# Moving two dense products, two splits and one group of transposes in a one-core recommendation kernel

## The reference, cut to what matters

```python
fm = emb_table[arange(26), cat_idx]                  # 26 looked-up rows of 128
dense = relu(relu(relu(x @ Wd1) @ Wd2) @ Wdf)        # biases left out here
Z = concat([fm, dense])                              # 27 x 128 per batch row
S = einsum("bie,bje->bij", Z, Z)                     # all products of pairs
x = concat([S[upper triangle], dense])               # 351 + 128
x = relu(x @ Wt1 + bt1)                              # 1024 wide
x = relu(x @ Wt2 + bt2)                              # 1024
x = relu(x @ Wt3 + bt3)                              # 512
x = relu(x @ Wt4 + bt4)                              # 256
out = sigmoid(x @ Wo + bo)
```

## Time and profile before

| quantity | value |
|---|---|
| median of three runs | 179.01 us (178.82 to 179.12) |
| span of the profiled execution, first to last instruction | 176.7 us |
| TensorE busy (matmul) | 160.0 us, 91% of the span |
| GpSimd busy | 102.6 us, 58% |
| VectorE busy | 71.1 us, 40% |
| ScalarE busy | 55.1 us, 31% |
| granted TensorE clock, mean | 0.981 |

### The profile page before, as it was taken

How to read it: one execution, slowest core, us unless ns; L and a number is a source line. 1 busy time by engine, 2 the same in 40 slices (tenths; PEclk the granted TensorE clock), 3 DMA queues, 4 the chain that set the end, 5 groups by cost and what they waited for, 6 DMA issues and landing times.

```text
span 176.7 us, 3837 instructions
## 1 busy us (share of the span) xinstructions
PE 160.0 (91%) x1681; PEld 115.5 (65%) x1681; DVE 71.1 (40%) x131; ACT 55.1 (31%) x93; POOL 102.6 (58%) x111
## 2 busy tenths in 40 slices
PE   1999997449889999999999999899999998999983
PEld 1334454225657878767787877677878776788971
DVE  5005358806869624162504122734121264321311
ACT  3378588431737403032211113231113041201110
POOL 3777777777778877777777777777777000000000
PEclk9999999975999999999999999999999999999999
DMA  2999556767987522222121212222221000000000
GB/s 52 318 389 270 163 157 178 207 194 242 342 235 261 165 51 57 54 58 55 49 59 48 58 50 59 48 59 52 56 56 52 15 4 0 0 0 4 0 0 0
DMA packets 6674, 18.18 MB, mean 103 GB/s; under 512 B 2309, under 2 KB 2441, under 8 KB 6530
## 3 DMA queue, kind: packets, MB, share of 16 engines
q1 hardware_dynamic: 3330, 11.12, 19.1%
q0 software_dynamic: 3328, 6.82, 15.3%
HBM read 17.93 MB, written 0.00 MB: 101 GB/s over the span
## 4 chain that ended last, share of the span: by engine, by line
PE 68%; POOL 13%; DVE 7%; issue 5%; DMA 3%; ACT 2%; DVEq 0%
PE mp L444 26%; POOL rows L312 13%; PE mp L465 10%; PE mp L413 9%; PE gp L377 6%; PE tp L421 5%; PE gp L367 4%; PE gp L483 3%; DVE xb L717 3%; PE mp L348 2%; DMA rows<-in_emb,row_of 2%; PE mp L506 1%; DVE raw L750 1%; PE gp L389 1%; ACT xth L581 1%
## 5 line engine op out<-in xcount | busy, mean ns | idle before, releaser
L312 POOL DMA_INDIRECT rows<-in_emb,row_of x104 | 101.7, 978 | 33.2 <-issue 29.6
L444 PE MATMUL mp<-w2l,a1h 128*128 128x512 f32 x64 | 26.7, 418 | 0.0
L444 PE MATMUL mp<-w2h,a1h 128*128 128x512 f32 x64 | 26.2, 410 | 0.0
L444 PE MATMUL mp<-w2h,a1l 128*128 128x512 f32 x64 | 25.5, 398 | 0.0
L570 ACT COPY zt<-gp 128x512 f32<-128x512 f32 x16 | 9.4, 586 | 46.6 <-PE gp L367 46.5
L367 PE MATMUL gp<-ident,rows 128*128 128x128 f32 x104 | 16.4, 278 | 5.4 <-DMA rows<-in_emb,row_of 5.4
L367 PEld LDWEIGHTS gp<-ident,rows 128*128 128x128 f32 x104 | 12.8, 142 | 10.4 <-DMA rows<-in_emb,row_of 6.5
L739 DVE TENSOR_TENSOR raw<-mp,bc 128x512 f32<-128x512 f32 x8 | 5.5, 690 | 29.4 <-PE mp L444 29.4
L377 PEld LDWEIGHTS gp<-zt 128*32 128x32 f32 x1024 | 11.4, 112 | 6.9 <-issue 6.0
L377 PE MATMUL gp<-zt 128*32 128x27 f32 x1024 | 13.5, 198 | 0.6 <-DVE zt L711 0.6
L444 PEld LDWEIGHTS mp<-w2h,a1l 128*128 128x128 f32 x64 | 12.1, 189 | 2.9 <-DVE a1l L733 0.9
(11 more groups left out here) (78 smaller groups left out, 231.2 us busy)
## 6 DMA issues: line engine op xcount, KB each, us to landing
w<-in_wt SPq DMA_DIRECT2D x13, 512.0 KB, 4.5
rows<-in_emb,row_of POOLq DMA_INDIRECT x104, 2.8
w<-in_wt SPq DMA_DIRECT2D x3, 468.0 KB
bc<-in_rows SPq DMA_DIRECT2D x1, 1024.0 KB, 7.0
wd_sb<-in_wd SPq DMA_DIRECT2D x1, 512.0 KB, 3.6
w1d<-in_wt SPq DMA_DIRECT2D x1, 512.0 KB, 6.7
bt<-in_rows SPq DMA_DIRECT2D x1, 512.0 KB, 9.2
wdf_sb<-in_wdf SPq DMA_DIRECT2D x1, 128.0 KB, 3.1
```

The lines of the kernel that those rows point to most:

```text
L312: pool.indirect_dma_start(out=rows[:, n % RING, :], out_offset=None, in_=emb.rearrange("c v e -> (c v) e"), in_offset=bass.IndirectOffsetO ...
L444: last = pe.matmul(mp[:, h, :], a[:, k, :], w[:, k, cols], start=(k == 0 and part == 0), stop=(k == M1 - 1 and part == 2))
```

## The change

The change has four parts.

1. **Dense products 6 and 7** go ahead of the transposes of tile 0's groups 6 and 7 on TensorE. On VectorE their bias additions go ahead of `features(0, 7)` and `turn_sums(0)`.
2. **Group 6** of each next tile goes from behind layer 3 into it, ahead of product 14. Group 7 stays behind layer 3.
3. **Group 5 and grams 2** go to earlier places in layer 3: ahead of products 4 and 10 in place of 10 and 16.
4. **Splits 9 and 10** go behind work of tile 0 on VectorE: split 9 behind `layer_1_sum(0, 1)`, and split 10 behind `layer_1_lo(0, 1)`.

```diff
-FEATURES_3 = [{10: [5]}] * 3 + [{}]
+FEATURES_3 = [{4: [5], 14: [6]}] * 3 + [{}]
 GRAMS_2 = [{10: 0, 34: 1}] * 3 + [{}]
-GRAMS_3 = [{16: 2}] * 3 + [{}]
+GRAMS_3 = [{10: 2}] * 3 + [{}]
...
             dense_products(5)
             grams(0, 2)
+            for m in range(6, 8):
+                dense_products(m)
             transpose_features(0, 6)
             transpose_features(0, 7)
             grams(0, 3)
-            dense_products(6)
-            dense_products(7)
             transpose_pairs(0)
...
                 layer_3(t)
-                transpose_features(t + 1, 6)
                 transpose_features(t + 1, 7)
                 turn(t, 4)
...
             split_lo(6)
+            dense_products_out(6)
+            dense_products_out(7)
             features(0, 7)
             turn_sums(0)
-            dense_products_out(6)
-            dense_products_out(7)
             pairs_lo(0)
...
                 layer_1_lo(t, 0)
+                layer_1_sum(t, 1)
                 if t == 0:
                     split_lo(9)
-                layer_1_sum(t, 1)
                 for n in range(PRODUCTS_2):
                     if n == TURN_1B:
+                        layer_1_lo(t, 1)
                         if t == 0:
                             split_lo(10)
-                        layer_1_lo(t, 1)
```

More of the change, by code:

```diff
@@ L650, in _ @@
                         layer_2_hi(t, 1)
-                features(t + 1, 6)
                 relu_3(t)
```

## The result

The changed kernel is **slower by 0.8%**: 180.0 us against 178.81 (medians of 12 runs each), a ratio of 1.0077 with a 95% interval of 1.0051 to 1.0103. The prediction was 178.7, which is 0.3 us faster. It gave chances of 0.4 for faster, 0.37 for no change and 0.23 for slower, and a range of 177.8 to 180.0, whose upper end the measured time just touches.

A forecast was written before the change was run, and what follows sets the result against it. TensorE was taken as the bound, with tile 1's gathers only 0.9 us ahead. Terms −0.1, −0.5, −0.17 and +0.54 gave −0.23, rounded to −0.3, so 179.01 − 0.3 = 178.7 us; range 177.8 to 180.0.

The forecast's parts named there:

- part 1's clock: End of tile 0's start-up: TensorE at full clock, making two transposes about 0.35 us and the grams 0.37 us shorter.
- Start-up's gain: Tile 0's layer 1 would start at 42.9 us, 2.4 us earlier; 1.4 to 1.7 with the clock low.
- half clock beyond 43 us: Sign in the new profile that would show the forecast wrong: TensorE still at its lower clock after 43 us.
- the sum: All terms over the span of 176.7 us: together −0.23, rounded to −0.3 us.
- 0.6 us of lead: End of tile 0's layer 3: −0.1 left after the wait for rows, and −0.5 from gathers coming earlier.
- the forecast's 0.54: Tiles 2 and 3: group 6's transposes inside layer 3 cost 2 × (0.44 − 0.17) = +0.54 us.
- The start-up gives nothing: Rival: clock stays low or falls again in tile 0's layer 1; 179.8 us, counted with slower cases, together 0.23.
- Layer 2 and the gathers: Tile 0's layers 2 and 3: TensorE's lead is partly lost waiting for tile 1's gathered rows.
- both forecast waits: Tile 0: TensorE waits until 50.4 us for tile 1's group 1, and 1.3 us inside layer 3 for group 6.
- Part 4: Splits 9 and 10 later: tile 0's second turn in layer 2 no longer waits for `raw`, winning 0.9 us.
- Layer 3: Group 6's four transposes inside cost 0.44 us, 0.17 won back behind; in tile 1 hidden by the wait for rows.
- The gathers' pace: GpSimd's gathers, stretched by VectorE's low parts, would come 0.5 us earlier, with −1.8 and +1.3 kept possible.

The follow-up runs named there:

- e4: The whole change plus four unused filler products around tile 0's group 6 and behind grams 3, against the kernel before: 179.14 us, ratio 1.0035.
- e8: The whole change plus two unused filler products behind grams 3 only, against the kernel before: 179.44 us, ratio 1.0027.
- e6: The kernel before plus three unused filler products ahead of tile 0's group 6 and one behind it, against the kernel before: 177.48 us, ratio 0.9920.
- e3: Only splits 9 and 10 moved one step back on VectorE, against the kernel before: 178.31 us, ratio 0.9968.
- e2: Only layer 3 changed (group 6 inside, group 5 and grams 2 earlier), against the kernel before: 179.81 us, ratio 1.0054.
- e5: The change with four filler products but layer 3 as before, group 6 behind it, against the kernel before: 177.31 us, ratio 0.9920.
- e7: The change with four filler products, low parts 7 to 14 replaced by one-input scaled copies, against the kernel before: 178.22 us, ratio 0.9966.

## Why the prediction was wrong

**The failed step is part 1's clock.** The text put the clock at full, "since the idle stretch ahead of the transposes shrinks from some 3.5 us to 1.6". It did shrink, and the clock fell all the same: TensorE was busy 2.50 of 4.6 us there and 2.91 of the next 6.9. The pauses of the kernel before and of the changed one, ahead of the fall:

```profile
36.42 0.66 PE L367 MATMUL gp<-ident,rows 128*128 128x128 f32 x4 [3.56 <-DMA rows<-in_emb,row_of]
```

```profile
36.05 0.66 PE L367 MATMUL gp<-ident,rows 128*128 128x128 f32 x4 [1.21 <-DMA rows<-in_emb,row_of]
38.36 0.44 PE L367 MATMUL gp<-ident,rows 128*128 128x128 f32 x2 [1.65 <-DMA rows<-in_emb,row_of]
```

The prediction looked at the longest pause alone, and it moved the very work that had brought the clock back before layer 1. Start-up's gain was 1.0 us in place of 2.4. Of the missing 1.4, 0.4 is tile 0's last gather, which landed at 38.31 in place of 37.89; nearly all the rest is grams and pairs at half clock. Counted from that landing, the gain is 1.4 us, the lower end of what the prediction gave for a low clock (1.4 to 1.7). What it left out is that the low stretch then goes on into layer 1: up to layer 2's first product it took 7.54 us in place of 5.28 (51.83 − 44.29 against 50.57 − 45.29), 2.3 us more. In the kernel before that product is

```profile
50.57 0.40 PE L444 MATMUL mp<-w2h,a1h 128*128 128x512 f32 x1
```

e4 and e8 show the cause, and e6 shows it in the kernel before. Of the prediction's own signs of being wrong, "half clock beyond 43 us" is the one that came.

**The clock is not all of it.** With the clock kept up, the change is still 0.35% slower than the kernel before (e4, 0.07 to 0.63%), where the sum had −0.3 us. The sum expected 0.6 us of lead at the end of tile 0's layer 3 and another 0.17 behind it. The trace of e4 has 0.44 there, and behind it 0.17 is lost in place of won (tile 1's sums start at 76.44, only 0.26 ahead of the 76.70 of before). The two later tiles cost 0.10 and 0.44, as much as the forecast's 0.54. So the forecast's second error lies between the end of tile 0's layer 3 and tile 1's layer 1, and its cause stays open; it is half a microsecond, which is also about the noise of one kernel's time.

**The rival that named it was priced wrongly.** "The start-up gives nothing" saw that a fall was possible, said that "up to some 2 us of it vanish in the waits", and folded it into the slower cases. Its 179.8 us came nearest of all, but by leaving out two terms that partly cancel: start-up did not give nothing but lost 1.25 us up to product 3, and the splits gave 0.87 of that back. The loss was 1.4 + 2.3 = 3.7 us against the planned start, more than all the waits together, so none was left and every cost behind them was paid in full.

**Layer 2 and the gathers: right, but not reached.** With TensorE late, group 1 was wanted at 52.6, long after its rows, and no wait for rows arose in tile 0's layers. With the clock up, both forecast waits stand in the traces, though in different kernels (e6: 1.25 us for group 1; e4: 0.49 for gather 49 inside layer 3), and in e8 together.

**Part 4: right in mechanism.** It took 0.87 us off the way from product 3 to product 4 (1.55 us before, 0.68 after), 0.9 being forecast. Alone it measured 0.4 to 0.6 us, barely clear of the noise (e3).

**Layer 3: right in size, wrong in where it was paid.** Since no wait for rows hid it, it was paid in tile 0 too. By the chains of the two profiles layer 3 took 0.42, 0.21 and 0.43 us more in tiles 0, 1 and 2 (in tile 1 of the kernel before, grams 2 had held it up by some 0.2). Behind it 0.29, 0.14 and 0 came back, where the prediction had 0.17 each time. Together that is 0.6 us, where the forecast price of 0.27 in each of three tiles would be 0.8. Without the lead it measured 0.54%, 1.0 us (e2, with an interval of 0.4 to 1.6).

**The gathers' pace: right in mechanism, not in phase.** They came 0.46 us later (gather 51 at 71.29) and not 0.5 earlier, with other low parts meeting other gathers, since everything from layer 1 on stood elsewhere. It did not matter: nobody waited. In the profiles of the kernels with true low parts, gather 51 was issued anywhere between 69.66 (e5) and 71.29: a spread of 1.6 us in what the prediction had laid out by hand to half a microsecond.

On the page SBUF — State Buffer of the Trainium skill, section "Who interferes with whom", a two-input VectorE instruction contends with GpSimd instructions that read SBUF, and it is inferred that writing descriptors is not hindered. The inference is not borne out for these gathers: they took 1.96 us in place of 0.94, and 0.9 us of time went when the low parts were shortened (e7). The prediction took the rule itself to speak against these gathers, but it need not: a gather takes its row numbers from `row_of`, which lies in SBUF, and so may count as a read. No run here separates the two.

What stays open is how a filler would do in other places, how much of the cost of group 6 is its transposes and how much TensorE's restart behind them, and why tile 0's last gather lands anywhere between 2.6 and 4.5 us after its issue in the profiles of these kernels (2.6 in e8, 2.97 in the kernel before, 4.48 in e3). That scatter of over a microsecond lies on the path of all of them.

## What to carry to other kernels

Before work is moved out of a stretch in which TensorE runs at its lower level, ask what else would bring the clock back: if nothing does, the stretch moves onto the next products. A few products that nobody reads, placed in a wait for data, gained 0.8% here and did as much as they did together with the reordered start-up and splits (e6 and e5, both 0.9920). A transfer or gather that is just in time belongs in the account of every lead: find its slack first, and put its consumer where it hides the wait, not where ten products stand behind it.

## What the runs showed of the hardware

- The granted clock fell to its lower level near 39 us in the changed kernel, although TensorE had made two dense products between 32.8 and 34.8 and its longest pause ahead of the fall was 1.65 us, against 3.56 in the kernel before. With the filler products of e4 it stayed at its upper level through that place and layer 1 (1.00 from 37.6 to 48).
- An indirect gather took GpSimd 0.94 us alone and 1.96 when it started just inside a 1.2 us subtraction of two SBUF operands.
- In the kernel before, the gathers issued between 64 and 69 us that were looked at singly landed 2.5 to 2.8 us after their issue, the one issued at 43.65, while weights and biases were being loaded, 6.7 us. In e8 the gather issued at 67.93 took 3.33.
